# Audio tower on one core: bias products that open the embedding accumulators, and the loads and roots around them

## What is computed

```python
x = layer_norm(x, g1, b1, 1e-6)                  # 448 x 1024
h = layer_norm(x @ W + b, g2, b2, 1e-6)          # W: 1024 x 512
h = h + attention(_layernorm(h))                 # 16 heads of 128, causal within a sequence of 7 rows
n = _layernorm(h)
scale = max(max(abs(n)) / 448, 1e-7)
h = h + (n / scale rounded to fp8) @ weight.T * weight_scale + bias   # as the reference has it
```

## Time and profile before

| what | us |
|---|---|
| median of 3 runs | 268.14 (267.61 to 269.72) |
| the profiled execution | 268.16 |
| its span, first to last instruction | 266.4 |
| busy within the span: TensorE | 256.4 (96%) |
| VectorE | 159.5 (60%) |
| ScalarE | 124.8 (47%) |
| mean granted TensorE clock | 0.991 of full |

### The profile page before, as it was taken

One profiled execution on the slowest core, in us unless ns is written; L12 is line 12 of the kernel. 1 busy time (PEld: TensorE's weight loads), 2 busy tenths in 40 slices (PEclk: granted clock), 3 DMA queues, 4 the chain that ended last, 5 costly groups with the idle time before them and its releaser, 6 DMA issues.

```text
span 266.4 us, 3864 instructions
## 1 busy us (share of the span) xinstructions
PE 256.4 (96%) x1434; PEld 219.8 (83%) x1434; DVE 159.5 (60%) x325; ACT 124.8 (47%) x215; POOL 0.2 (0%) x4
## 2 busy tenths in 40 slices
PE   7799999899899999999999999999999999999994
PEld 6344446898799999999999999999999999998672
DVE  5268996833926903872394269138722967934884
ACT  2666964354534542534362435325443642546680
POOL 0000000000000000000000000000000000000000
PEclk9999999999999999999999999999999999999888
DMA  6999030033071053023305210530240020000004
GB/s 180 332 277 387 11 119 0 2 123 113 0 253 65 2 197 118 1 60 137 118 0 171 64 80 0 197 118 0 43 153 0 2 79 0 2 0 0 0 4 138
DMA packets 7627, 23.63 MB, mean 89 GB/s; under 512 B 1261, under 2 KB 1725, under 8 KB 7488
## 3 DMA queue, kind: packets, MB, share of 16 engines
q1 hardware_dynamic: 7616, 23.48, 26.9%
HBM read 22.56 MB, written 0.92 MB: 88 GB/s over the span
## 4 chain that ended last, share of the span: by engine, by line
PE 88%; DMA 4%; DVE 3%; SPq 2%; issue 1%; ACT 1%; DVEq 0%; ACTq 0%
PE bank L315 14%; PE bank L317 14%; PE bank L316 14%; PE acc L459 9%; PE acc L350 9%; PE bank L434 5%; PE bank L443 5%; PE acc L463 4%; DMA tokw_raw<-tok_w 4%; PE acc L653 3%; PE bank L449 3%; PE bank L426 2%; SPq L248 2%; PE bank L523 2%; PE bank L639 1%; PE bank L339 1%
## 5 line engine op out<-in xcount | busy, mean ns | idle before, releaser
L315 PE MATMUL bank<-ht_hi,qkvw_hi 128*128 128x448 f32 (+1 forms) x192 | 69.4, 362 | 0.9 <-issue 0.9
L317 PE MATMUL bank<-ht_hi,qkvw_lo 128*128 128x448 f32 (+1 forms) x192 | 69.1, 360 | 0.0
L316 PE MATMUL bank<-ht_lo,qkvw_hi 128*128 128x448 f32 (+1 forms) x192 | 69.0, 359 | 0.0
L948 DVE TENSOR_TENSOR qkvw_lo<-raw_qkv,qkvw_hi 128x1536 fp32r<-128x1536 f32 x16 | 28.1, 1754 | 35.6 <-ACT qkvw_hi L685 35.6
L315 PEld LDWEIGHTS bank<-ht_hi,qkvw_hi 128*128 128x128 f32 x192 | 36.1, 188 | 3.9 <-issue 1.3
L317 PEld LDWEIGHTS bank<-ht_hi,qkvw_lo 128*128 128x128 f32 x192 | 36.1, 188 | 2.7
L316 PEld LDWEIGHTS bank<-ht_lo,qkvw_hi 128*128 128x128 f32 x192 | 36.1, 188 | 2.6
L350 PE MATMUL acc<-tokw_raw,xt 128*112 128x512 f32 x64 | 29.7, 600 | 1.7 <-DMA tokw_raw<-tok_w 1.3
L685 ACT CAST qkvw_hi<-raw_qkv 128x1536 fp32r<-128x1536 f32 x16 | 23.5, 1477 | 0.0
L350 PEld LDWEIGHTS acc<-tokw_raw,xt 128*112 128x112 f32 x64 | 10.4, 176 | 15.4 <-issue 9.6
L1154 DVE COPY prob_t<-bank 112x448 f32<-112x448 f32 x8 | 5.0, 625 | 29.0 <-PE bank L426 29.0
(11 more groups left out here) (148 smaller groups left out, 396.5 us busy)
## 6 DMA issues: line engine op xcount, KB each, us to landing
raw_qkv<-heads_w SPq DMA_DIRECT2D x16, 768.0 KB, 4.3
raw_out<-heads_w SPq DMA_DIRECT2D x16, 256.0 KB, 4.5
tokw_raw<-tok_w SPq DMA_DIRECT2D x4, 512.0 KB, 7.4
x_in<-patches SPq DMA_DIRECT2D x3, 448.0 KB, 11.2
ffnw_raw<-ffn_w SPq DMA_DIRECT2D x1, 1024.0 KB, 16.4
out<-h_sb SPq DMA_DIRECT2D x3, 224.0 KB, 2.6
x_in<-patches SPq DMA_DIRECT2D x2, 224.0 KB, 3.0
g_row<-tok_g SPq DMA_DIRECT2D x1, 224.0 KB, 10.7
```

Source lines behind the costliest of these rows:

```text
L315: nc.tensor.matmul(ps, hi, whi, start=first, stop=False, skip_group_check=True)
L316: nc.tensor.matmul(ps, hi, wlo, start=False, stop=False, skip_group_check=True)
L317: return nc.tensor.matmul(ps, lo, whi, start=False, stop=last, skip_group_check=True)
L948: return nc.vector.tensor_tensor(dst, src, hi.bitcast(F32), ALU.subtract)
```

## The change

- The bias. Its split form and the closing products are gone. `first_ones` (112 x 112) is zero but for row 0, which is one; `tok_b_rows` (112 x 512) is cleared and gets the bias in row 0 by a load of 2 KB. Their product in float32 opens each accumulator (`begin_with_bias`): for tiles 1 to 3 ahead of the first patch transposes, for tile 0 behind them. `embed` adds to it and closes with its last product.
- VectorE clears the two tiles ahead of the others; SyncE waits for that and loads the bias after the first patches, ahead of `ident`.
- 6 warming products at the start, not 14; they wait for the first clear alone.
- The patches of tile 1 are loaded between weight pieces 0 and 1, not behind piece 1.
- The transposes of tile 1 stand before product 6 of tile 0, not behind it. The orders of the other transposes stay.
- The norm of tile 0's stream takes its root from ScalarE too (12 columns in `ROOTS`); `rsqrt` with the integer guess is gone. In `rsqrt_from_roots` one tensor_scalar becomes a scalar_tensor_tensor.
- ScalarE's order from tile 2 on: `patch_evacuate(2)` ahead of `normalise(3)`, the new root, `take_root(TILES + 1)` and `split_qkv(0, 0)` behind; `patch_evacuate(3)` ahead of `normalise_stream(1)`; `split_qkv(0, 1)` and `split_out(0, 0)` behind `stream_evacuate(0)`; one root ahead of `stream_evacuate(1)`.
- VectorE takes the statistics of tile 3 ahead of its wait for the rows `g2` and `b2`.

The core of the diff:

```diff
-WARM_START, WARM_STATS, WARM_RSTD, WARM_SCALE = 14, 2, 3, 3
+WARM_START, WARM_STATS, WARM_RSTD, WARM_SCALE = 6, 2, 3, 3
...
-ROOTS = {0: LN_EPS, 1: LN_EPS, 2: LN_EPS, 3: LN_EPS, TILES: LN_EPS, 2 * TILES + 1: NORM_EPS, TILES + 2: LN_EPS,
-         2 * TILES + 2: NORM_EPS, TILES + 3: LN_EPS, 2 * TILES + 3: NORM_EPS}
+ROOTS = {0: LN_EPS, 1: LN_EPS, 2: LN_EPS, 3: LN_EPS, TILES: LN_EPS, 2 * TILES: NORM_EPS, TILES + 1: LN_EPS,
+         2 * TILES + 1: NORM_EPS, TILES + 2: LN_EPS, 2 * TILES + 2: NORM_EPS, TILES + 3: LN_EPS,
+         2 * TILES + 3: NORM_EPS}
...
             for c, landed in ((slice(0, 512), x_landed[0]), (slice(512, IN_DIM), x0_rest_landed)):
                 load(x_in[:, 0, c], patches[0][:, c], landed)
+            sp.wait_ge(bias_cleared, 2)
+            load(tok_b_rows[0:1, :], tok_b[0:1, :], tok_b_landed)
             load(ident_sb[:], ident, ident_landed)
             load(g1_col[:], tok_g1, cols_landed)
             load(b1_col[:], tok_b1, cols_landed)
             load_tokw(0)
-            load(tok_b_raw[:], tok_b, tok_b_landed)
+            load(x_in[:, 1, :], patches[1], x_landed[1])
             load_tokw(1)
-            load(x_in[:, 1, :], patches[1], x_landed[1])
...
+            def begin_with_bias(t):
+                nc.tensor.matmul(acc[t][0:TR, :], first_ones[:], tok_b_rows[:], start=True, stop=False,
+                                 skip_group_check=True)
+
+            def embed(t, ahead_of):
+                for k in range(KIN):
+                    if k in ahead_of:
+                        ahead_of[k]()
...
-                                     start=(k == 0), stop=False, skip_group_check=True)
...
+                    last = nc.tensor.matmul(acc[t][0:TR, :], xt[:, t % 2, k * TR:(k + 1) * TR], tokw_raw[:, k, :],
+                                            start=False, stop=(k == KIN - 1), skip_group_check=True)
+                last.then_inc(tok_ps, 1)
...
-            pe.wait_ge(ones_ok, 2)
+            pe.wait_ge(ones_ok, 1)
             keep_warm(WARM_START, acc[TILES - 1])
+            pe.wait_ge(bias_ones_ok, 1)
+            pe.wait_ge(tok_b_landed, 16)
+            for t in range(1, TILES):
+                begin_with_bias(t)
             patch_transposes(0)
...
+            begin_with_bias(0)
+            embed(0, {KIN - 2: lambda: patch_transposes(1)})
+            embed(1, {KIN // 2: lambda: patch_transposes(2)})
+            embed(2, {KIN // 2: lambda: patch_transposes(3)})
+            stream_transposes(0)
+            embed(3, {KIN // 2: lambda: stream_transposes(1)})
             stream_transposes(2)
...
             patch_evacuate(0)
-            act.wait_ge(tok_b_landed, 16)
-            hi_part(tok_b_split[:], tok_b_raw[:]).then_inc(tok_b_hi_ok, 1)
             take_root(1)
             normalise(1)
             patch_evacuate(1, between=lambda: take_root(2))
             normalise(2)
             take_root(3)
             take_root(TILES)
+            patch_evacuate(2)
             normalise(3)
-            patch_evacuate(2)
+            take_root(2 * TILES)
+            take_root(TILES + 1)
             split_qkv(0, 0)
+            normalise_stream(0)
+            patch_evacuate(3, between=lambda: take_root(2 * TILES + 1))
+            normalise_stream(1)
+            stream_evacuate(0)
+            take_root(TILES + 2)
             split_qkv(0, 1)
             split_out(0, 0)
-            normalise_stream(0)
-            take_root(2 * TILES + 1)
-            patch_evacuate(3)
-            stream_evacuate(0)
-            take_root(TILES + 2)
-            normalise_stream(1)
+            take_root(2 * TILES + 2)
             stream_evacuate(1)
-            take_root(2 * TILES + 2)
             normalise_stream(2)
             stream_evacuate(2)
...
-                    done[c] = mark(nc.vector.tensor_scalar(n, y, y, v, ALU.mult, ALU.mult))
+                    done[c] = mark(nc.vector.scalar_tensor_tensor(out=n, in0=y, scalar=v, in1=y,
+                                                                  op0=ALU.mult, op1=ALU.mult))
...
             nc.vector.memset(ones_sb[:], 1.0).then_inc(ones_ok, 1)
+            nc.vector.memset(first_ones[:], 0.0).then_inc(bias_cleared, 1)
+            nc.vector.memset(tok_b_rows[:], 0.0).then_inc(bias_cleared, 1)
+            dve.wait_ge(bias_cleared, 1)
+            nc.vector.memset(first_ones[0:1, :], 1.0).then_inc(bias_ones_ok, 1)
```

More of the change, by code:

```diff
@@ L133, in audio_tower @@
         ones_sb = sb("ones_sb", [TR, TR])
+        first_ones = sb("first_ones", [TR, TR])
         ones_r = sb("ones_r", [B_LO + 1, TR], F32R)
@@ L148, in audio_tower @@
         tok_b_landed = sem("tok_b_landed")
-        tok_b_hi_ok = sem("tok_b_hi_ok")
-        tok_b_lo_ok = sem("tok_b_lo_ok")
+        bias_cleared = sem("bias_cleared")
+        bias_ones_ok = sem("bias_ones_ok")
         rows_landed = sem("rows_landed")
@@ L342, in patch_transposes @@
                         mm.then_inc(xt_ps, 1)
-            def embed(t, half, within=None):
-                for k in range(half * KIN // 2, (half + 1) * KIN // 2):
+            def begin_with_bias(t):
[5 more added lines that the diff above has]
+                        ahead_of[k]()
                     for i, (first_chunk, _) in enumerate(TOKW_PIECES):
@@ L877, in take_last_roots @@
                 nc.scalar.activation(last_root[:], moments[:, LAST:LAST + TILES, 1], ACT.Sqrt,
-                                     bias=eps_4[:, 1:2], scale=4.0).then_inc(last_root_ok, 1)
+                                     bias=eps_4[:, NORM_ROOT:NORM_ROOT + 1], scale=4.0).then_inc(last_root_ok, 1)
             def scale_rows(t):
@@ L956, in moments_of, with need_moments @@
                 link(last)
[L957 to L966, removed]
+                nc.vector.bn_aggr(moments[:, c, :], stats[:, c, 0:len(parts), :]).then_inc(variance_ok, 1)
+            def need_moments(c):
+                dve.wait_ge(variance_ok, list(ROOTS).index(c) + 1)
             def rsqrt_from_roots(columns, between=None):
@@ L990, in rsqrt_from_roots @@
                                                                   op0=ALU.add, op1=ALU.mult))
[L991 to L1017, removed]
                 return max(done.values())
@@ L1027, in patch_moments @@
                 dve.wait_ge(x_landed[t], 16)
-                return moments_of(t, [x_in[:, t, i * 512:(i + 1) * 512] for i in range(IN_DIM // 512)],
-                                  x0_rest_landed if t == 0 else None)
+                moments_of(t, [x_in[:, t, i * 512:(i + 1) * 512] for i in range(IN_DIM // 512)],
+                           x0_rest_landed if t == 0 else None)
             def stream_lo(t):
@@ L1039, in stream_lo @@
                         ht_hi[:, :, c]).then_inc(ht_lo_ok, 1)
-            stream_step = {}
             def stream_norms(t, own, between=None, patch=None):
-                columns, step = [], 0
+                columns = []
                 if t is not None:
@@ L1050, in stream_norms @@
                     dve.wait_ge(tok_ps, t + 1)
-                    step = moments_of(c, [acc[t][0:TR, :]])
-                    need_moments(c, step)
+                    moments_of(c, [acc[t][0:TR, :]])
+                    need_moments(c)
                     centred_step = mark(nc.vector.scalar_tensor_tensor(
@@ L1056, in stream_norms @@
                         op0=ALU.subtract, op1=ALU.mult))
-                    columns.append((c, LN_EPS))
+                    columns.append(c)
                 if patch is not None:
-                    step = max(s for s in (step, patch[1], 0) if s is not None)
-                    columns.append((patch[0], LN_EPS))
+                    columns.append(patch)
                 if own is not None:
-                    step = max(s for s in (step, stream_step[own], 0) if s is not None)
-                    columns.append((2 * TILES + own, NORM_EPS))
-                need(rsqrt(columns, step, between))
+                    columns.append(2 * TILES + own)
+                need(rsqrt_from_roots(columns, between))
                 if patch is not None:
-                    negative_mean_scaled(patch[0]).then_inc(x_scaled, 1)
+                    negative_mean_scaled(patch).then_inc(x_scaled, 1)
                 if own is not None and own < TILES - 1:
@@ L1097, in _ @@
                 nc.vector.memset(eps_4[:, i:i + 1], 4.0 * eps).then_inc(eps_ok, 1)
-            need(rsqrt([(0, LN_EPS)], patch_moments(0)))
+            patch_moments(0)
+            need(rsqrt_from_roots([0]))
             negative_mean_scaled(0).then_inc(x_scaled, 1)
@@ L1101, in _ @@
                                     rstd[:, 0:1], ALU.subtract, ALU.mult).then_inc(x0_half_normed, 1)
-            need(rsqrt([(1, LN_EPS)], patch_moments(1)))
-            negative_mean_scaled(1).then_inc(x_scaled, 1)
-            def bias_lo():
-                b = slice(B_LO, B_LO + 1)
-                dve.wait_ge(tok_b_hi_ok, 1)
```

(11 more changed lines are left out.)

32 lines of the change are left out of this document (4 added, 28 removed).

## The result

| | before | after |
|---|---|---|
| median, 19 executions each | 267.61 us | 266.01 us |
| profiled execution (span) | 268.16 (266.4) | 266.61 (264.8) |
| ratio after to before | | 0.9943, 95% interval 0.9922 to 0.9963 |

The changed kernel is 0.6% faster, 1.5 us by the ratio. The forecast time, 265.9 us, is 0.1 from the median, and that closeness is luck: two errors cancel. The gain was forecast at 2.3 us and is 1.5 to 1.6. Between the two profiles it is 1.55 us, and those can be followed stretch by stretch.

The account below looks back on a forecast made before the run. TensorE, holding 88% of the chain, was taken to bound the kernel; 0.66 us at the start, 1.56 from bias products and 0.1 from Newton steps made 2.3 off 268.16, so 265.9 us, range 265.0 to 267.3.

Parts of the forecast that it names:

- The sign and the size class: Whole kernel: faster, by 2.3 us to 265.9; chance 0.68 for the same within about 1%, faster 0.27, slower 0.05.
- The bias products: TensorE from tile 2's patch transposes to tile 3's end: removing closing bias products and delays behind them saves 1.56 us.
- The Newton step: VectorE's chain before the last stream's transposes: a cheaper second step saves 0.05 to 0.11 us each, 0.1 in all.
- The root of tile 0 and the splits: ScalarE's new root (0.30 us) and head weight splits (1.44 each) fall in stretches with slack and cost nothing.
- The start: Up to tile 2's patch transposes: these begin at 21.75 us instead of 22.41, a gain of 0.66 (0.3 to 1.0).
- The prediction's own sign of being wrong: Any of: first transposes after 9 us, TensorE waiting on ScalarE between 22 and 41, tile 3's end after 42.
- W: Time at which TensorE reaches full pace; opening bias products end at 4.83 + W/2 us, free up to W = 8.2.
- the clock is late: Rival at the start: full pace comes late, at 11 us tile 0 ends 1.3 later, 267.2; chance 0.14 with queue.
- the free 8.95: Latest start in us of the first patch transposes that leaves embedding call 2 at 12.3 us.
- the landing of weight piece 1: Load that embedding call 2 of tile 0 waits for: lands at 12.3 us, bounds 11.9 and 12.5.
- the rule that a landing comes when 0.88 MB more have moved: Start's loads: a piece lands once 0.88 MB beyond the queue's sum has moved; gave weight piece 1 at 11.9 us.
- The end's clock: Rival near 251.5 us: low-clock stretch misses this work, 1.6 us faster, 264.3 (chance 0.07), or a second, 267.5 (0.04).

Follow-up runs that it names:

- e3: Kernel before with its four closing bias products left out, loads and splits kept; ratio to the kernel before 0.9942.
- e13: Changed kernel with the old split bias (33 rows) as each tile's opening product, loaded ahead of `ident`, and 15 warming products; 264.96 us, ratio to the kernel before 0.9909.
- e2: Changed kernel with 9 warming products instead of 6; median 264.68 us, ratio to the kernel before 0.9907.
- e12: e2 with ScalarE's normalisation of tile 3 ahead of the evacuation of tile 2 again; last stream's transposes start at 45.74 us.
- e1: Changed kernel with 14 warming products instead of 6; ratio to the kernel before 0.9940.
- e8: e2 with the patches of tile 1 loaded behind weight piece 1 again; last stream's transposes start at 46.33 us.
- e10: Kernel before with its 33-row bias load moved from behind weight piece 0 to ahead of `ident`; ratio to the kernel before 1.0022.
- e11: e4 with the 2 KB bias row load moved behind weight piece 0; patches of tile 1 land at 9.72 us, of tile 2 at 15.94.
- e4: Changed kernel with its four opening bias products left out; ratio to the kernel before 0.9928.
- e9: Kernel before with its 33-row bias load replaced by a clearing and two one-row loads at the same place; ratio to the kernel before 1.0084.

## Why the prediction was right, and where it was not

**The sign and the size class** are right: faster by less than 1%, on the forecast mechanism, TensorE's own work.

**The bias products**, 1.56 us from tile 2's transposes on: right, as the chain shows, and e3 agrees with it (2.2 us for all four calls against a sum of 2.1, with two other effects in it).

**The Newton step**, 0.05 to 0.11 us each: L973 now takes 0.219 us where L985 took 0.272, 0.053 each, and the chain through VectorE is 0.11 shorter. Right.

```profile
L973 DVE SCALAR_TENSOR_TENSOR newton<-rstd,vscaled 112x1 f32<-112x1 f32 x12 | 2.5, 219 | 0.3
```

The root of tile 0 and the splits cost nothing, as said, and no wait of TensorE on ScalarE appears between 22 and 41 us.

**The start** is where it failed, and 0.66 us became 0.09. The prediction's own sign of being wrong, first transposes after 9 us, came true (9.62), and so embedding call 2 (12.96 us, not 12.3), tile 0's last call (18.88, not 18.2) and the last transposes (47.42, not 46.9) are late as well. Two steps were wrong, and they would have moved the time in opposite directions. First, that full pace comes at W = 8.2 us or earlier, so that the bias products are free. W was 9.4, and the rival called *the clock is late* (0.14 together with a late queue) is what happened. Its own pricing held: the bias products were to end at 4.83 + W/2 = 9.5 us and did at 9.62; 0.6 to 0.7 later than the free 8.95 puts embedding call 2 at 12.9 to 13.0 instead of 12.3, and the chain has it at 11.24 + 1.72 = 12.96. The error was the weighing. To count anew from the first bias product fits the profiles (4.6 and 5.2 us, above); but the sum took the 3.7 us of one profile as fixed, got 8.1 us, and called the start free on a margin of 0.1 us. The ten starts without a gap spread from 3.6 to 6.2, and 3.7 is near their low end; 4.4 plus that spread is 8.0 to 10.6.

Second, the landing of weight piece 1 at 12.3 us (bounds 11.9 to 12.5). It is there at 10.55 us or before in e13, at 10.72 in e2, 10.98 in e12 and 11.78 in e1, all below the lower bound, so the rule that a landing comes when 0.88 MB more have moved came out 0.5 to 1.8 us too late. Tile 2's patches were forecast at 17.3 us and landed at 15.85. Had the load been the limit at 12.3, e2 would have shown a wait behind its second embedding call. The late pace hid this error: it made TensorE the bound before the load was.

The rule of the Trainium skill that the prediction set against the edit (TensorE: Matmul & The Clock Gate, Why this matters for your kernels), to keep the engine continuously busy at the start, agrees with these profiles: with a gap full pace comes 7.8 us or more after the first product, without one after at most 6.2.

**The end's clock.** The rival priced a missed low stretch at 1.6 us and did not show the working. The changed kernel's profile has exactly that, a granted clock of 1.00 throughout:

```profile
251.00:252.00 1.00, 0.96 (x10) 1.00 0.00 0
252.00:253.00 1.00, 0.15 (x1) 1.00 0.00 0
...
249.47 0.53 PE bank L634 x4
...
250.03 0.62 DVE xt L1211
...
252.31 0.40 DVE xq_t L1239
...
252.85 2.19 PE acc L648 x8
```

From the first statistics of the end to the last copy it takes 17.55 us against 17.68: 0.13 less. When the transposes are fast, VectorE's chain to the quantised tile (250.03 to 252.71) holds the end instead, and TensorE's faster work waits. A price near 1.6 needs TensorE's pieces to stay on the chain. In e1 and e13, where the clock fell for a part of this stretch as it did in the kernel before, it took 17.89 and 18.03 us, so a low stretch costs 0.1 to 0.5 us in these profiles, not 1.6.

**The base.** The sum was made against one profiled execution that stood at the first median of three; more executions put the kernel before 0.55 us lower. That, and a gain 0.7 too large, put 266.01 within 0.1 of 265.9.

**Open.** Why the loads of the changed kernel land earlier than in the kernel before. The patches of tile 2 are there at 15.85 us against 17.19; neither the order of patches and weights (e8) nor the place and size of the bias load (e10, e11, e13) gives more than 0.8 us of it. Nor is it in every execution: in e1, with the loads of the changed kernel, they land at 17.21, and in seven other profiles of that order between 15.23 and 15.87. Differences of some tenths between single profiles tell nothing here. It decides nothing in the changed kernel, since TensorE arrives later than the loads.

## What to carry to other kernels

Work put into an idle start is free only at the pace the engine has then: price it at the slow pace until a profile shows otherwise, and leave no gap between what warms the engine and what follows. The moment of full pace in one profile is one draw from a spread, here of 2.6 us. When two limits lie within a microsecond of each other, say what the time is if either is wrong; here, by their profiles, removing the products (e4) gave less than keeping them and adding three throw-away ones in front (e2, e8, e12). A price summed over one engine's instructions holds only until the next engine's chain takes over.

## What the runs showed of the hardware

- In the first microseconds the column of the granted clock reads 1.00 though every record takes twice its time (0.85 us for 512 columns against 0.43 later). At the start the durations tell the clock, the column doesn't.
- Without a gap full pace (2.4 GHz) came 3.6 to 6.2 us after the first product, in ten profiles. Behind 2.6 us of work at half pace and a gap of 0.6 us it came 7.8 and 8.4 us after the first, 4.6 and 5.2 after the first behind the gap; with a gap of 3.3 and 3.4 us, 5.2 and 5.1 after the first behind it.
- The gaps of 0.7 us in the kernel before and 1.3 us in e13, once at full pace, did not bring the slow pace back: the patch transposes behind them stand 0.10 us apart.
- A scalar_tensor_tensor of one element a row with its scalar read from memory takes 0.219 us; with an immediate 0.159, and a tensor_scalar with two scalars from memory 0.272.
- Two loads of one row (2 KB) behind the first weight piece brought the last weight piece 3.1 us later (e9); one of them, in another kernel, at most 0.4 us (e11), no more than such landings scatter.
